# A wait inside each projection in place of a pacing wait in front of it, in a fused sequence-mixing and expert kernel

## Chip, cores and metric

The kernel runs on one core of one Trainium2 chip, as one program. The metric is the device time in microseconds of one execution; lower is better.

## What is computed

The input x is (8, 1024, 256) in fp32. Two blocks, each behind a layer norm over the 256 columns and added to x:

```python
def attn(x):                               # (the sequence-mixing half)
    xp, z = split(x @ w_in)                # 256 -> 2 x 512
    xc = silu(causal_conv(xp, 4 taps) + conv_b)
    h_t = 0.9 * h_{t-1} + 0.1 * (xc_t @ w_B)   # state of 16
    return ((h @ w_C) * silu(z)) @ w_out   # "out projection", 512 -> 256

def ffn(x):
    idx = top_2(x[:, 0, :] @ Wr + br)      # per sequence, from its first token
    h = gelu(x @ W1[idx] + b1[idx])        # two experts, 256 -> 256 each
    return mean over the two of (h @ W2[idx] + b2[idx])   # "down projection"

x = x + attn(layernorm(x))
x = x + ffn(layernorm(x))
```

## The kernel before

The 8,192 tokens are cut into 16 chunks of 512 tokens. The kernel is a pipeline over chunks: step s does the sequence mixing of chunk a = s, the out projection of chunk o = s - 1 and the expert half of chunk f = s - 2. Steps 4 to 13 are a hardware loop over pairs of steps, the others are written out. Each engine has its own program of steps; semaphores that count up order them.

Each matrix product is done in split precision: both operands are kept as a high part (fp32r) and the rest, and three products (hi by hi, lo by hi, hi by lo) add up in one bank of PSUM. A product is two instructions of TensorE: a weight load (LDWEIGHTS, 128 x 128, the stationary operand) and a matmul that streams the moving operand. A wait in front of a product is carried by its weight load, an increment by its matmul. The profile shows weight loads as engine PEld and matmuls as PE.

There are two sizes of product. In xp and z (both in_proj), up, state_in and state_out the moving operand is 512 tokens ("long" products, 128x512). In the out projection (out_proj) and the down projection (down) the stationary operand is a tile of 128 tokens and the moving one is a 256-column weight ("short" products, 128x256). These two go through tokens(h, j, ...), where h is a half of the chunk (two tiles of 128 tokens) and j one of four slices of the contraction: six short products for each call, lines 1419 to 1421. A projection is 2 halves x 4 slices x 6 = 48 short products. The out projection runs in one piece; of down the first 36 run in one piece and the last 12 behind state_out.

The order of TensorE in one step is: xp (24 long), out_proj(o, 0) and out_proj(o, 1) (48 short), z (24 long), up (24 long), state_in (8 long), down(f, 0) and the first half of down(f, 1) (36 short), state_out (4 long), the rest of down(f, 1) (12 short). Every other step has six tiny products of the router (score) at its start.

In front of 15 out projections and 15 down projections stands behind(tail, count). The third-last product of the long stream in front counts up a semaphore (x_tail, state_tail or up_tail). TensorE first counts up a semaphore of its own that nobody reads (paced), then waits for the third-last product's end, and then issues PACE = 2 more increments of paced before it comes to the first weight load of the projection.

Of the kernel before, what the change touches and what calls it, by code (L numbers as in the profile page):

```python
# [16 lines left out]
SQ = 32  # L17
QUADS = P // SQ
EARLY = 2
PACE = 2  # L20


def build_block(nc, x, w_in, conv_w, conv_b, w_B, w_C, w_out, Wr, br, W1, b1, W2, b2, out):
# [10 lines left out]
    JD = DI // P  # L34
    JF = TOP_K * KD
# [7 lines left out]
    with ExitStack() as ctx:  # L43
# [3 lines left out]
        def sem(name):  # L47
            return ctx.enter_context(nc.semaphore(name))
# [43 lines left out]
        w_out_hi, w_out_lo = sb("w_out_hi", [P, JD, D], F32R), sb("w_out_lo", [P, JD, D], F32R)  # L92
        w2_hi, w2_lo = sb("w2_hi", [P, TOP_K, KD * D], F32R), sb("w2_lo", [P, TOP_K, KD * D], F32R)
# [6 lines left out]
        y_hi, y_lo = sb("y_hi", [P, JD, CH], F32R), sb("y_lo", [P, JD, CH], F32R)  # L100
        hid_hi, hid_lo = sb("hid_hi", [P, JF, CH], F32R), sb("hid_lo", [P, JF, CH], F32R)
# [35 lines left out]
        t1_hi, t1_lo = sem("t1_hi"), sem("t1_lo")  # L137
        half_turned = sem("half_turned")
        half_hi, half_lo = sem("half_hi"), sem("half_lo")
        t2_hi, t2_lo = sem("t2_hi"), sem("t2_lo")  # L140
# [25 lines left out]
        up_ready = sem("up_ready")  # L166
# [6 lines left out]


        passed = sem("passed")
        x_tail, state_tail, up_tail = sem("x_tail"), sem("state_tail"), sem("up_tail")
        paced = sem("paced")


        raw_in = gate[:].rearrange("p j c -> p (j c)").rearrange("p (k c) -> p k c", k=KD)  # L180
# [90 lines left out]
        def has_attn(s):  # L271
            return not isinstance(s, int) or s <= LAST
# [964 lines left out]
        def _(pe):  # L1237
# [49 lines left out]
                    nc.tensor.transpose(blk[0][:, k * P:(k + 1) * P], by_token(normed2, 0)[:, k * P:(k + 1) * P],  # L1287
                                        ident[:]).then_inc(token_turned, 1)

            def project(bank, whi, wlo, his, los, ready, c, sem_out, third_last=None, between=None):  # L1290

                dst = bank[:]
                for k in range(KD):
                    if ready is not None:
                        pe.wait_ge(ready[0], c * KD + k + 1)
                    mm(dst, whi(k), his(k), start=(k == 0), stop=False)  # L1296
                    ins = mm(dst, wlo(k), his(k), start=False, stop=False)  # L1297
                    if k == 0 and between is not None:
                        between()
                if third_last is not None:  # L1300
                    ins.then_inc(third_last, 1)
                for k in range(KD):
                    if ready is not None:
                        pe.wait_ge(ready[1], c * KD + k + 1)
                    ins = mm(dst, whi(k), los(k), start=False, stop=(k == KD - 1))  # L1305
                ins.then_inc(sem_out, 1)

            def in_proj(a, j, part, bank, sem_out, between=None):
                cols = slice(part * DI + j * P, part * DI + (j + 1) * P)
                project(bank, lambda k: w_in_hi[:, k, cols], lambda k: w_in_lo[:, k, cols],  # L1310
                        lambda k: xn1(a)[0][:, k, :], lambda k: xn1(a)[1][:, k, :],
                        (t1_hi, t1_lo) if part == 0 and j == 0 else None, a, sem_out,
                        x_tail if part == 0 and j == JD - 1 else None, between)

            def last_tap(a, j):
                return a * JD * HALO + (j // 2) * 2 * HALO + 2 * (HALO - 1) + j % 2 + 1
# [53 lines left out]
            def up(s, f, q, seq):  # L1370
                for j in range(JF):
                    if q == 0 and j % KD == 0:
                        pe.wait_ge(w1_lo_set, seq * TOP_K + j // KD + 1)
                    if has_attn(s):
                        pe.wait_ge(gate_set, s * JD + j + 1)
                    elif has_out(s):
                        pe.wait_ge(y_set, NC * JD - JD + j + 1)
                    else:
                        pe.wait_ge(gelu_set, f * JF - JF + j + 1)
                    t, m = j // KD, j % KD  # L1380
                    project(blk[j], lambda k: w1_hi[:, t, k * D + m * P:k * D + (m + 1) * P],
                            lambda k: w1_lo[:, t, k * D + m * P:k * D + (m + 1) * P],
                            lambda k: xn2(f)[0][:, k, :], lambda k: xn2(f)[1][:, k, :],
                            (t2_hi, t2_lo) if j == 0 else None, f, up_ready,
                            up_tail if j == JF - 1 and not has_attn(s) else None)

            def up_first():
                his, los = xn2(0)
# [21 lines left out]
                            lambda k: w1_lo[:, 1, k * D + m * P:k * D + (m + 1) * P],  # L1410
                            lambda k: his[:, k, :], lambda k: los[:, k, :], None, 0, up_ready)

            def tokens(h, j, last, his, los, whi, wlo):


                for n in range(2):
                    rows = slice((2 * h + n) * P, (2 * h + n + 1) * P)
                    dst = tok[h][:, n * D:(n + 1) * D]
                    mm(dst, his[:, j, rows], whi, start=(j == 0 and n == 0), stop=False, skip_group_check=True)  # L1419
                    mm(dst, his[:, j, rows], wlo, start=False, stop=False, skip_group_check=True)  # L1420
                    ins = mm(dst, los[:, j, rows], whi, start=False, stop=(last and n == 1), skip_group_check=True)  # L1421
                return ins

            def behind(tail, count):
                pe.sem_inc(paced, 1)
                pe.wait_ge(tail, count)
                for _ in range(PACE):
                    pe.sem_inc(paced, 1)

            def down_tile(f, n, dst, js=range(JF)):  # L1430
                rows = slice(n * P, (n + 1) * P)
# [5 lines left out]
                if js[-1] == JF - 1:  # L1437
                    ins.then_inc(down_ready, 1)

            def down(f, h, js=range(JF), tail=None):  # L1440
                for j in js:
                    if h == 0:
                        pe.wait_ge(g_lo, f * JF + j + 1)
                        if isinstance(f, int) and f == LAST - 1 and j % KD == 0:
                            pe.wait_ge(w2_lo_set, LAST // 2 * TOP_K + j // KD + 1)
                    if j == 0 and tail is not None:
                        behind(*tail)
                    t, cols = j // KD, slice(j % KD * D, (j % KD + 1) * D)
                    ins = tokens(h, j, j == JF - 1, hid_hi, hid_lo, w2_hi[:, t, cols], w2_lo[:, t, cols])
                if js[-1] == JF - 1:  # L1450
                    ins.then_inc(down_ready, 1)

            def out_proj(o, h, tail=None):
                pe.wait_ge(done, o * 2 + h + 1)
                for j in range(JD):
                    if h == 0:
                        if isinstance(o, int) and o == LAST and j:
                            pe.wait_ge(last_y_lo, j)
                        else:
                            pe.wait_ge(y_lo_set, o * JD + j + 1)  # L1460
                    if j == 0 and tail is not None:
                        behind(*tail)
                    ins = tokens(h, j, j == JD - 1, y_hi, y_lo, w_out_hi[:, j, :], w_out_lo[:, j, :])
                ins.then_inc(mixed, 1)

            def state_in(a):
                bank = u_bank(a)
                for j in range(JD):
                    pe.wait_ge(xc_hi_set, a * JD + j + 1)
                    mm(bank[:], b_mix[:, j, :], xc_hi[:, j, :], start=(j == 0), stop=False)  # L1470
                for j in range(JD):
                    pe.wait_ge(xc_lo_set, a * JD + JD if isinstance(a, int) and a < 3 else a * JD + j + 1)
                    ins = mm(bank[:], b_mix[:, j, :], xc_lo[:, j, :], start=False, stop=(j == JD - 1))  # L1473
                    if j == JD - 3:
                        ins.then_inc(state_tail, 1)
                ins.then_inc(u_ready, 1)

            def state_out(a, s, js=range(JD)):
# [41 lines left out]
            def opening():  # L1520
# [22 lines left out]
                for j in (1, 2, 3):  # L1543
                    xp(2, j)
                pe.wait_ge(z_out_lo_set, 3)
                out_proj(0, 0, (x_tail, 3))
                out_proj(0, 1)
                state_in(1)
                z(2, (0, 1))
# [6 lines left out]
                up_first()  # L1556
                state_in(2)
                pe.wait_ge(y_set, 2 * JD)
                out_proj(1, 0, (state_tail, 3))
                out_proj(1, 1)  # L1560
                pe.wait_ge(w2_lo_set, TOP_K)
                pe.wait_ge(mid_set, 3)
# [8 lines left out]
            def step(s, q, half):  # L1571
# [4 lines left out]
                    for j in range(JD):  # L1576
                        xp(a, j)
                if has_out(s):
                    out_proj(o, 0, (x_tail, a + 1) if has_attn(s) else None)
                    out_proj(o, 1)  # L1580
                if has_attn(s):
                    z(a)
# [10 lines left out]
                else:  # L1593
                    pe.wait_ge(done, f * 2 + 3)
                if not has_out(s):
                    down(f, 0, (0, 1, 2), (up_tail, 2))
                    pe.wait_ge(done, f * 2 + 4)
                    down_tile(f, 2, tok[1][:, 0:D], (0, 1, 2))
                    down(f, 0, (3,))
                    down_tile(f, 2, tok[1][:, 0:D], (3,))  # L1600
                    down_tile(f, 3, turn[0][:, 0:D])
                    return
                if isinstance(s, int) and s == NC:
                    down(f, 0, (0, 1, 2), (up_tail, 1))
                    down(f, 1, (0, 1))
                    down(f, 0, (3,))
                    turns2(o)
                    down(f, 1, (2, 3))
                    return
                down(f, 0, range(JF), (state_tail, a + 1))  # L1610
                down(f, 1, (0, 1))
                if has_attn(s):
                    state_out(a, s)
# [30 lines left out]
```

## Time and profile before

| | us |
|---|---|
| median of 3 runs | 507.03 |
| lowest, highest | 506.91, 507.4 |
| the profiled execution | 507.05 |
| its span, first to last instruction | 505.0 |
| TensorE (PE) busy | 499.6 |
| weight loads (PEld) busy | 438.9 |
| VectorE, ScalarE, GpSimd busy | 452.7, 400.5, 348.1 |

Times of a timeline are us from the start of the span. A matmul's duration in the profile holds its passage through the array, so neighbours overlap: the distance from one start to the next is what a product costs the stream, and the duration is when its result is there. The granted TensorE clock is 1.00 of the upper level over the whole span.

### The profile page before, as it was taken

The numbers are of one execution on the slowest core, as the hardware profiler recorded it, in microseconds if no ns is written. First come the engines' busy times: TensorE is split into PE (matmuls) and PEld (weight loads), VectorE is DVE, ScalarE is ACT, GpSimd is POOL, SyncE is SP. The second block draws the span as 40 slices with busy tenths as digits, with TensorE's granted clock in tenths as the row PEclk, the third lists the DMA queues.
The fourth block names the chain that finished last, engine by engine and source line by source line (L and its number), as shares of the span: only waits on it lengthen the run. The fifth ranks groups of instructions, "written<-read, shape, count | busy, mean of one in ns | idle before, by whom it ended". The sixth has DMA issues, their size and how long they took to land.

```text
span 505.0 us, 9913 instructions
## 1 busy us (share of the span) xinstructions
PE 499.6 (99%) x3026; PEld 438.9 (87%) x3026; DVE 452.7 (90%) x896; ACT 400.5 (79%) x692; POOL 348.1 (69%) x390
## 2 busy tenths in 40 slices
PE   7999999999999999999999999999999999999997
PEld 7888799888888888888889888888888888888997
DVE  6999999999998899989999899998999989996773
ACT  4986959878869788697887969879797888969454
POOL 4959597559693796928969197783977649673391
PEclk9999999999999999999999999999999999999999
DMA  8940105335251532606235170542614333130102
GB/s 255 298 183 5 38 1 178 115 127 168 69 184 42 166 125 83 208 15 196 80 125 166 42 224 25 166 125 86 205 42 139 110 126 126 55 113 1 42 2 84
DMA packets 53379, 57.28 MB, mean 113 GB/s; under 512 B 8682, under 2 KB 49642, under 8 KB 53226
## 3 DMA queue, kind: packets, MB, share of 16 engines
q1 hardware_dynamic: 51498, 56.67, 34.8%
q10 hardware_dynamic: 1856, 0.31, 0.3%
q8 instruction: 12, 0.20, 0.2%
q14 instruction: 13, 0.11, 0.1%
HBM read 35.46 MB, written 21.50 MB: 113 GB/s over the span
## 4 chain that ended last, share of the span: by engine, by line
PE 98%; DVE 1%; DMA 1%; issue 0%; DVEq 0%
PE blk L1296 16%; PE blk L1297 16%; PE blk L1305 16%; PE tok L1419 12%; PE tok L1421 11%; PE tok L1420 11%; PE blk L1494 3%; PE turn L1470 3%; PE turn L1473 3%; PE turn L1243 1%; PE tok L1296 1%; PE tok L1297 1%; PE tok L1305 1%; DMA x_mid<-in_L_attn_x 1%; DVE stats_t L917 0%; DVE normed L934 0%
## 5 line engine op out<-in xcount | busy, mean ns | idle before, releaser
L992 DVE SCALAR_TENSOR_TENSOR conv<-blk,tap_w,conv 128x512 f32<-128x512 f32 x192 | 130.1, 740 | 7.3 <-ACT conv L683 6.4
L488 POOL TENSOR_TENSOR y_lo<-gate,y_hi 128x512 fp32r<-128x512 f32 x57 | 72.2, 1297 | 36.0 <-ACT y_hi L611 35.9
L1296 PE MATMUL blk<-xn_hi,w_in_hi 128*128 128x512 f32 x228 | 89.5, 392 | 0.0
L1297 PE MATMUL blk<-xn_hi,w_in_lo 128*128 128x512 f32 x228 | 89.0, 391 | 0.0
L453 POOL TENSOR_TENSOR xc_lo<-conv,xc_hi 128x512 fp32r<-128x512 f32 x60 | 73.1, 1236 | 7.7 <-ACT xc_hi L611 7.6
L1419 PE MATMUL tok<-w_out_hi,y_hi 128*128 128x256 f32 x256 | 72.3, 282 | 0.0
L1421 PE MATMUL tok<-w_out_hi,y_lo 128*128 128x256 f32 x256 | 70.8, 277 | 0.0
L1420 PE MATMUL tok<-w_out_lo,y_hi 128*128 128x256 f32 x256 | 70.7, 276 | 0.0
L1305 PE MATMUL blk<-xn_lo,w_in_hi 128*128 128x512 f32 x228 | 70.3, 390 | 0.0
L1419 PE MATMUL tok<-w_hi,hid_hi 128*128 128x256 f32 x248 | 70.3, 283 | 0.0
L1420 PE MATMUL tok<-w_lo,hid_hi 128*128 128x256 f32 x248 | 68.9, 278 | 0.0
L1421 PE MATMUL tok<-w_hi,hid_lo 128*128 128x256 f32 x248 | 68.8, 278 | 0.0
L683 ACT ACTIVATE conv<-blk,tap_b,tap_w 128x512 f32<-128x512 f32 x64 | 49.2, 778 | 24.8 <-PE blk L1305 21.6
L689 ACT ACTIVATE conv<-conv 128x512 f32<-128x512 f32 x64 | 39.4, 630 | 30.4 <-DVE conv L992 29.4
L861 DVE TENSOR_TENSOR hid_lo<-hid,hid_hi 128x512 fp32r<-128x512 f32 x64 | 45.1, 731 | 16.0 <-ACT hid_hi L611 15.7
L498 POOL TENSOR_TENSOR x_mid<-x_mid,b_sel 128x256 f32<-128x256 f32 x60 | 45.7, 793 | 13.3 <-DVE hid_lo L861 11.3
L1419 PEld LDWEIGHTS tok<-w_out_hi,y_hi 128*128 128x128 f32 x256 | 48.0, 188 | 3.8 <-issue 3.6
L1305 PEld LDWEIGHTS blk<-xn_lo,w_in_hi 128*128 128x128 f32 x228 | 42.8, 188 | 9.1
L1419 PEld LDWEIGHTS tok<-w_hi,hid_hi 128*128 128x128 f32 x248 | 46.5, 188 | 4.4 <-issue 3.9
L1297 PEld LDWEIGHTS blk<-xn_hi,w_in_lo 128*128 128x128 f32 x228 | 42.8, 188 | 8.1
L1296 PEld LDWEIGHTS blk<-xn_hi,w_in_hi 128*128 128x128 f32 x228 | 42.8, 188 | 8.1
L1296 PE MATMUL blk<-xn_hi,w_hi 128*128 128x512 f32 x124 | 48.4, 390 | 0.0
(189 smaller groups left out, 1319.4 us busy)
## 6 DMA issues: line engine op xcount, KB each, us to landing
spill<-normed SPq DMA_DIRECT2D x25, 512.0 KB, 2.8
normed<-spill SPq DMA_DIRECT2D x100, 128.0 KB, 2.9
out<-x_mid SPq DMA_DIRECT2D x30, 256.0 KB, 2.3
x_mid<-in_L_attn_x SPq DMA_DIRECT2D x29, 256.0 KB, 2.8
x_in<-in_L_attn_x SPq DMA_DIRECT2D x14, 512.0 KB, 4.6
w_all<-in_L_ffn_W SPq DMA_DIRECT2D x2, 2048.0 KB, 11.3
b_all<-in_L_ffn_b SPq DMA_DIRECT2D x1, 1024.0 KB, 13.7
gate<-in_L_attn_w_in SPq DMA_DIRECT2D x2, 256.0 KB, 4.8
```

The costliest lines, as they stand in the source:

```text
L453: nc.gpsimd.tensor_tensor(xc_lo[:, j, :], conv[:, j, 0:CH], xc_hi[:, j, :].bitcast(F32), ALU.subtract).then_inc(xc_lo_set, 1)
L488: nc.gpsimd.tensor_tensor(y_lo[:, j, :], gate_of(o, j), y_hi[:, j, :].bitcast(F32), ALU.subtract).then_inc(y_lo_set, 1)
L498: ins = nc.gpsimd.tensor_tensor(mid(f, q)[:, n, :], mid(f, q)[:, n, :], b2_sel[:], ALU.add)
L683: nc.scalar.activation(conv[:, j, HALO:HALO + CH], blk[j][:], ACT.Identity, bias=tap_b[:, j:j + 1], scale=tap_w[:, j, 0:1]).then_inc(tap_f ...
L861: return nc.vector.tensor_tensor(dst, src, hi.bitcast(F32), ALU.subtract)
L992: nc.vector.scalar_tensor_tensor(cols, blk[j][:], tap_w[:, j, t:t + 1], cols, ALU.mult, ALU.add).then_inc(tap_added, 1)
L1296: mm(dst, whi(k), his(k), start=(k == 0), stop=False)
L1297: ins = mm(dst, wlo(k), his(k), start=False, stop=False)
L1305: ins = mm(dst, whi(k), los(k), start=False, stop=(k == KD - 1))
L1419: mm(dst, his[:, j, rows], whi, start=(j == 0 and n == 0), stop=False, skip_group_check=True)
L1420: mm(dst, his[:, j, rows], wlo, start=False, stop=False, skip_group_check=True)
L1421: ins = mm(dst, los[:, j, rows], whi, start=False, stop=(last and n == 1), skip_group_check=True)
```

## The change

The pacing goes: the three tail semaphores, paced, PACE and behind(), and the arguments that carried them. In its place tokens() gets a semaphore and a count for its first call of a projection (h = 0, j = 0). The first product counts the semaphore up at its end, and the fifth product (the second of the second tile) waits for that count. Products 2, 3 and 4 are issued before that wait. This is done for all 16 out projections (first_out) and all 16 down projections (first_down), so also for the first down and the last out projection, which had no pacing.

```diff
-PACE = 2
...
-        x_tail, state_tail, up_tail = sem("x_tail"), sem("state_tail"), sem("up_tail")
-        paced = sem("paced")
+        first_out, first_down = sem("first_out"), sem("first_down")
...
-            def project(bank, whi, wlo, his, los, ready, c, sem_out, third_last=None, between=None):
+            def project(bank, whi, wlo, his, los, ready, c, sem_out, between=None):
...
-                    ins = mm(dst, wlo(k), his(k), start=False, stop=False)
+                    mm(dst, wlo(k), his(k), start=False, stop=False)
...
-                if third_last is not None:
-                    ins.then_inc(third_last, 1)
...
-            def tokens(h, j, last, his, los, whi, wlo):
+            def tokens(h, j, last, his, los, whi, wlo, first=None, count=None):
...
-                    mm(dst, his[:, j, rows], whi, start=(j == 0 and n == 0), stop=False, skip_group_check=True)
+                    ins = mm(dst, his[:, j, rows], whi, start=(j == 0 and n == 0), stop=False, skip_group_check=True)
+                    if first is not None and n == 0:
+                        ins.then_inc(first, 1)
+                    if first is not None and n == 1:
+                        pe.wait_ge(first, count)
                     mm(dst, his[:, j, rows], wlo, start=False, stop=False, skip_group_check=True)
...
-            def behind(tail, count):
-                pe.sem_inc(paced, 1)
-                pe.wait_ge(tail, count)
-                for _ in range(PACE):
-                    pe.sem_inc(paced, 1)
...
-            def down(f, h, js=range(JF), tail=None):
+            def down(f, h, js=range(JF)):
...
-                    if j == 0 and tail is not None:
-                        behind(*tail)
...
-                    ins = tokens(h, j, j == JF - 1, hid_hi, hid_lo, w2_hi[:, t, cols], w2_lo[:, t, cols])
+                    ins = tokens(h, j, j == JF - 1, hid_hi, hid_lo, w2_hi[:, t, cols], w2_lo[:, t, cols],
+                                 *((first_down, f + 1) if h == 0 and j == 0 else ()))
...
-                    ins = tokens(h, j, j == JD - 1, y_hi, y_lo, w_out_hi[:, j, :], w_out_lo[:, j, :])
+                    ins = tokens(h, j, j == JD - 1, y_hi, y_lo, w_out_hi[:, j, :], w_out_lo[:, j, :],
+                                 *((first_out, o + 1) if h == 0 and j == 0 else ()))
...
-                    if j == JD - 3:
-                        ins.then_inc(state_tail, 1)
...
-                out_proj(0, 0, (x_tail, 3))
+                out_proj(0, 0)
...
-                down(f, 0, range(JF), (state_tail, a + 1))
+                down(f, 0)
```

The other callers change in the same way.

## Rows read from the trace of the kernel before

**Rows 1.** The page, busy time of the engines (share of the span) and instructions.

```profile
PE 499.6 (99%) x3026; PEld 438.9 (87%) x3026; DVE 452.7 (90%) x896; ACT 400.5 (79%) x692; POOL 348.1 (69%) x390
```

**Rows 2.** The page, chain of work that ended last, by engine.

```profile
PE 98%; DVE 1%; DMA 1%; issue 0%; DVEq 0%
```

**Rows 3.** The waits: who waited for whom, total us, times, longest us.

```profile
PEld tok L1419 <- issue: 7.5, 30, 0.4
```

**Rows 4.** Timeline, matmuls, xp, out projection and z of one step: start us, us.

```profile
201.26 0.61 PE L1305 MATMUL blk<-xn_lo,w_in_hi 128*128 128x512 f32 x2
...
203.98 0.62 PE L1305 MATMUL blk<-xn_lo,w_in_hi 128*128 128x512 f32 x2
204.45 0.36 PE L1419 MATMUL tok<-w_out_hi,y_hi 128*128 128x256 f32 x1
204.64 0.28 PE L1420 MATMUL tok<-w_out_lo,y_hi 128*128 128x256 f32 x1
...
205.56 0.28 PE L1419 MATMUL tok<-w_out_hi,y_hi 128*128 128x256 f32 x1
...
209.64 0.28 PE L1419 MATMUL tok<-w_out_hi,y_hi 128*128 128x256 f32 x1
...
209.98 0.40 PE L1296 MATMUL blk<-xn_hi,w_in_hi 128*128 128x512 f32 x1
```

**Rows 5.** Timeline, weight loads at the start of the same out projection.

```profile
203.99 0.19 PEld L1305 LDWEIGHTS blk<-xn_lo,w_in_hi 128*128 128x128 f32 x1
204.41 0.19 PEld L1419 LDWEIGHTS tok<-w_out_hi,y_hi 128*128 128x128 f32 x1 [0.24 <-issue]
```

**Rows 6.** Timeline, matmuls, state_in, 36 products of down, state_out.

```profile
221.80 1.07 PE L1473 MATMUL turn<-xc_lo,b_mix 128*128 128x512 f32 x4
222.71 0.36 PE L1419 MATMUL tok<-w_hi,hid_hi 128*128 128x256 f32 x1
222.91 0.28 PE L1420 MATMUL tok<-w_lo,hid_hi 128*128 128x256 f32 x1
...
226.88 1.09 PE L1494 MATMUL blk<-state_mix,c_mix 128*128 128x512 f32 x4
```

**Rows 7.** Timeline, matmuls, last 12 products of down behind state_out.

```profile
227.80 0.28 PE L1419 MATMUL tok<-w_hi,hid_hi 128*128 128x256 f32 x1
227.92 0.28 PE L1420 MATMUL tok<-w_lo,hid_hi 128*128 128x256 f32 x1
...
229.22 0.17 PE L1502 MATMUL turn<-spread_hi,token_hi 128*1 128x8 f32 x1
```

**Rows 8.** Timeline, matmuls, the 36 products of down in step 15.

```profile
465.65 0.36 PE L1419 MATMUL tok<-w_hi,hid_hi 128*128 128x256 f32 x1
465.84 0.28 PE L1420 MATMUL tok<-w_lo,hid_hi 128*128 128x256 f32 x1
...
469.96 0.63 PE L1494 MATMUL blk<-state_mix,c_mix 128*128 128x512 f32 x2
```

**Rows 9.** Timeline, a late operand in front of state_out, and down behind it.

```profile
134.61 1.01 DVE L861 TENSOR_TENSOR state_mix<-state,state_mix 64x512 fp32r<-64x512 f32 x1 [0.20 <-ACT state_mix L611]
...
135.68 0.30 PEld L1494 LDWEIGHTS blk<-state_mix,c_mix 128*128 128x128 f32 x2
...
136.72 0.28 PE L1419 MATMUL tok<-w_hi,hid_hi 128*128 128x256 f32 x1
...
137.96 0.28 PE L1421 MATMUL tok<-w_hi,hid_lo 128*128 128x256 f32 x1
```

**Rows 10.** Timeline, matmuls, the last out projection.

```profile
476.29 0.39 PE L1419 MATMUL tok<-w_out_hi,y_hi 128*128 128x256 f32 x1
476.51 0.28 PE L1420 MATMUL tok<-w_out_lo,y_hi 128*128 128x256 f32 x1
...
477.92 0.28 PE L1420 MATMUL tok<-w_out_lo,y_hi 128*128 128x256 f32 x1
```

More of the change, by code:

```diff
@@ L1311, in in_proj @@
                         lambda k: xn1(a)[0][:, k, :], lambda k: xn1(a)[1][:, k, :],
-                        (t1_hi, t1_lo) if part == 0 and j == 0 else None, a, sem_out,
-                        x_tail if part == 0 and j == JD - 1 else None, between)
+                        (t1_hi, t1_lo) if part == 0 and j == 0 else None, a, sem_out, between)
             def last_tap(a, j):
@@ L1383, in up @@
                             lambda k: xn2(f)[0][:, k, :], lambda k: xn2(f)[1][:, k, :],
-                            (t2_hi, t2_lo) if j == 0 else None, f, up_ready,
-                            up_tail if j == JF - 1 and not has_attn(s) else None)
+                            (t2_hi, t2_lo) if j == 0 else None, f, up_ready)
             def up_first():
@@ L1445, in down, with out_proj @@
                             pe.wait_ge(w2_lo_set, LAST // 2 * TOP_K + j // KD + 1)
-                    if j == 0 and tail is not None:
-                        behind(*tail)
                     t, cols = j // KD, slice(j % KD * D, (j % KD + 1) * D)
-                    ins = tokens(h, j, j == JF - 1, hid_hi, hid_lo, w2_hi[:, t, cols], w2_lo[:, t, cols])
+                    ins = tokens(h, j, j == JF - 1, hid_hi, hid_lo, w2_hi[:, t, cols], w2_lo[:, t, cols],
+                                 *((first_down, f + 1) if h == 0 and j == 0 else ()))
                 if js[-1] == JF - 1:
                     ins.then_inc(down_ready, 1)
-            def out_proj(o, h, tail=None):
+            def out_proj(o, h):
                 pe.wait_ge(done, o * 2 + h + 1)
@@ L1460, in out_proj @@
                             pe.wait_ge(y_lo_set, o * JD + j + 1)
-                    if j == 0 and tail is not None:
-                        behind(*tail)
-                    ins = tokens(h, j, j == JD - 1, y_hi, y_lo, w_out_hi[:, j, :], w_out_lo[:, j, :])
+                    ins = tokens(h, j, j == JD - 1, y_hi, y_lo, w_out_hi[:, j, :], w_out_lo[:, j, :],
+                                 *((first_out, o + 1) if h == 0 and j == 0 else ()))
                 ins.then_inc(mixed, 1)
@@ L1558, in opening @@
                 pe.wait_ge(y_set, 2 * JD)
-                out_proj(1, 0, (state_tail, 3))
+                out_proj(1, 0)
                 out_proj(1, 1)
@@ L1578, in step @@
                 if has_out(s):
-                    out_proj(o, 0, (x_tail, a + 1) if has_attn(s) else None)
+                    out_proj(o, 0)
                     out_proj(o, 1)
@@ L1595, in step @@
                 if not has_out(s):
-                    down(f, 0, (0, 1, 2), (up_tail, 2))
+                    down(f, 0, (0, 1, 2))
                     pe.wait_ge(done, f * 2 + 4)
@@ L1603, in step @@
                 if isinstance(s, int) and s == NC:
-                    down(f, 0, (0, 1, 2), (up_tail, 1))
+                    down(f, 0, (0, 1, 2))
                     down(f, 1, (0, 1))
```

## Prediction, made before the changed kernel was run

> **What bounds the kernel.** I read the busy shares first. TensorE is busy for 499.6 of 505.0 us [rows 1], and the chain that ended last is 98% TensorE [rows 2]. No other engine sets the pace over a stretch of any length, so a nanosecond gained or lost between two products is gained or lost at the end. Then I asked the waits for the weight-load side. The only wait that returns all through the run is the one that the change touches: the load of the first L1419 product was idle 30 times, 7.5 us in total, with no data to blame ("issue") [rows 3]. That is 0.25 us each, but the load side is always idle for 0.04 us per 512-column product (loads of 0.19 us, products 0.227 us apart), and products overlap loads. So the 7.5 us are not the price. The price has to be read from product starts.
>
> The timeline gives two units. Products of 512 columns start 2.72 / 12 = 0.2267 us apart (201.26 to 203.98), and products of 256 columns start 4.08 / 36 = 0.1133 us apart (205.56 to 209.64) [rows 4]. From the start of the L1305 pair at 203.98 to the first product of z at 209.98 there are two long and 48 short products. They should take 2 x 0.2267 + 48 x 0.1133 = 5.89 us and took 6.00. **Each paced out projection loses 0.11 us.** It is visible where: the first load starts 0.42 us after the load before it [rows 5], and the second product starts 0.19 us after the first [rows 4]. For a paced down projection: from 221.80 to 226.88 there are four long and 36 short products, 0.907 + 4.080 = 4.987 us, and it took 5.08. **0.09 us** [rows 6]. I take 0.10 for each of the 30.
>
> The second thing to see is that short products have two rhythms. The last 12 products of down(f, 1) follow directly on the four long products of state_out, with nothing held, and take 229.22 - 227.80 = 1.42 us, 0.118 us each [rows 7]. Such entries come 13 times behind state_out; 12 of them are at 0.118 and one at 0.113. Of the 30 paced entries, 29 settle at 0.113 within about five products, and one stays slow for all its 36 products: (469.96 - 465.84) / 35 = 0.118 [rows 8]. The difference of 0.0045 us is per product, so a slow out projection of 48 loses 0.216 us and a slow run of 36 loses 0.16. The granted clock is at its upper level (2.4 GHz) in all of these, so it is not the clock. The pace buys the quick rhythm with 0.10 us.
>
> **The change, part by part.**
>
> 1. Removed: the wait for the third-last product and two semaphore instructions behind it, at 30 places; with them goes the late first load. Three of the 30 started late for their data anyway (the one behind 130.5 us by 0.2 us), so 27 x 0.10 = 2.7 us can come back at most. The increments on the third-last products cost nothing and save nothing: the rhythm of 0.227 runs through them [rows 4].
>
> 2. What an entry costs with nothing held: the first short product behind state_out starts at 227.80, where the fourth long one started at about 226.88 + 3 x 0.229 = 227.57, so after 0.23 us, and the next follows 0.12 later [rows 6, 7]. So 0.003 us, and 3 x 0.0045 = 0.014 us for the three intervals up to the fourth product if they are slow.
>
> 3. Added: the fifth product's load waits for the first product's end, 16 out and 16 down projections. A short product lasts 0.28 us in these rows [rows 7]. A load that waits for another engine starts about 0.06 us after that end: DVE ended at 134.61 + 1.01 = 135.62, the load came at 135.68 [rows 9]. So the fifth load is free 0.34 us after the first product's start. Without the wait it would start with the fourth product, at 3 x 0.1133 = 0.34 in the quick rhythm or 3 x 0.118 = 0.354 in the slow one. The wait ends just when its load is due. Lower bound of its cost: nothing. Upper bound: a full restart as now, 0.19 - 0.11 = 0.08 us [rows 4], if the release is later than that of another engine. The value is near the lower one, as 0.34 against 0.34 says; I take 0.01, and 0.01 for settling. Behind the waiting load stand only TensorE's own products; while it waits, products 2 to 4 run and hide it. The computing of its count is an instruction more that those three products cover too. The increment rides on a product, as above: nothing.
>
> 4. The rhythm afterwards, the disputed term. Rows 9 are the 13th entry behind state_out: there the first load of state_out was held for the DVE until 135.68, and the 12 short products that follow go from 136.72 to 137.96 in 1.24 / 11 = 0.113. A load held in the midst of the first out projection, at 43.3 us, also left 0.113 behind it. Against that, one held at 476.29 was followed by 0.118 (476.51 to 477.92, 12 intervals) [rows 10]. With the paced entries that makes 31 of 33 held starts quick, and 12 of 12 unheld entries behind a stream of long products slow. (Of three unheld entries behind transposes two were slow and one quick.) The fifth load is held, if barely; so I take quick.
>
> The sum: 27 x (0.10 - 0.003 - 0.014 - 0.02) = 27 x 0.063 = 1.7 us, and 0.1 us of the slow 36 at 465.65 if that one turns quick. 1.8 us in all. The profiled execution took 507.05 us (505.0 of span and 2.05 around it), the median is 507.03: 507.0 - 1.8 = **505.2**. The first down projection and the last out projection are not paced now and get the new wait: nothing for 0.01 us each.
>
> **Rivals.**
>
> *B, the wait is over before it can act, and the projections run slow.* It is the same arithmetic read strictly: a wait whose end comes at 0.34 holds nothing that is due at 0.354, so the entry is an unheld one, and 12 of 12 of those were slow. All other held starts in this trace were held by 0.1 us or more. Then an out projection costs 0.216 + 0.003 in place of 0.10 (+0.12) and a down projection's 36 products 0.16 + 0.003 (+0.065): 15 x 0.185 = 2.8 us, plus some 0.2 for the three sites whose pace was hidden. **510.0.** It decides if the fifth load starts with the fourth product and the rhythm behind it is 0.118. Against it: the 12 entries follow only four long products, which were themselves not yet in their rhythm (0.23 apart), where the entries here follow 24 or 56 settled ones; none of those is unheld in this trace.
>
> *C, the two kinds part.* Outs slow and downs quick: 15 x 0.12 - 15 x 0.06 = +0.9, 507.9. Outs quick and downs slow: 15 x 0.065 - 15 x 0.06 = +0.1, 507.1. The rhythm follows from small offsets, and the two kinds have different streams in front, so it can be.
>
> *D, the rhythm is quick from the first product and the wait costs nothing.* Then all of it comes back: 27 x 0.10 + 0.16 = 2.9 us, **504.1**. The mechanism is that a load is always covered by the product before it, so that nothing but the late first load was lost. The Trainium skill says so: "TensorE: Matmul & The Clock Gate", in its sections on the gap between issues and on LDWEIGHTS, puts a load of 128 columns at about 107 ns and a 256-column product at about 109, which leaves a load no way to be the bound. The trace does not agree where nothing is held, with 0.118 in rows 7 against 0.113 in rows 4, and so this gets little.
>
> *E, the fifth load comes late and the loss moves from the first product to the fifth.* 0.08 + 0.037 = 0.12 us a site against 0.10 now: 30 x 0.02 = +0.6, 507.6.
>
> **Chances.** The forecast A 0.36, D 0.12, B 0.33, C 0.12, E 0.07. About 0.2% (1.0 us) is what a measurement of this kernel can tell from no change. A and D are faster, save for a small part of A with a smaller gain: 0.47. C with quick outs, E and that part: 0.18. B and the rest of C: 0.35. The predicted time is that of A; its own range is 504.6 to 506.0. B is too likely to be left out, so the range goes from D to B: 504.0 to 510.1.
>
> **What would show it.** In the profile of the changed kernel, the idle time of L1419's loads on "issue" (7.5 us, 30 times) goes. The first short product starts 0.23 us behind the last long one and the second 0.12 after it: step 2. The fifth product's load starts within 0.36 us of the first product: step 3; at 0.42 or more it is E. From the tenth to the last product of an out projection the mean interval is 0.1133 (A, D) or 0.118 (B): step 4. The forecast is wrong if that interval is 0.118 while the fifth load was not late.

## The result and the profile after

The changed kernel takes 508.76 us (508.58 to 510.16, 8 runs) against 507.21 for the kernel before in the same comparison (506.47 to 507.75, 8 runs). The ratio is 1.0033, with a 95% interval of 1.0023 to 1.0043: a third of a per cent slower. The profiled execution took 508.75 us with a span of 507.0, 2.0 more than before. The granted clock is 1.00 throughout, as before.

The page of the changed kernel, busy time of the engines, answers to [rows 1]. TensorE is still the bound, with 2.3 us more of busy time for the same 3026 products:

```profile
PE 501.9 (99%) x3026; PEld 446.5 (88%) x3026; DVE 452.0 (89%) x896; ACT 401.2 (79%) x692; POOL 347.7 (69%) x390
```

Its waits no longer have the line of [rows 3], L1419's loads on "issue". The timeline shows the entry of the same out projection as in [rows 4], matmuls first: start us, duration us.

```profile
204.38 0.61 PE L1301 MATMUL blk<-xn_lo,w_in_hi 128*128 128x512 f32 x2
204.83 0.28 PE L1413 MATMUL tok<-w_out_hi,y_hi 128*128 128x256 f32 x1
204.95 0.28 PE L1418 MATMUL tok<-w_out_lo,y_hi 128*128 128x256 f32 x1
205.07 0.28 PE L1419 MATMUL tok<-w_out_hi,y_lo 128*128 128x256 f32 x1
205.19 0.28 PE L1413 MATMUL tok<-w_out_hi,y_hi 128*128 128x256 f32 x1
205.31 0.28 PE L1418 MATMUL tok<-w_out_lo,y_hi 128*128 128x256 f32 x1
...
210.49 0.40 PE L1294 MATMUL blk<-xn_hi,w_in_hi 128*128 128x512 f32 x1
```

Its weight loads, where before there was the late one of [rows 5]:

```profile
204.61 0.19 PEld L1413 LDWEIGHTS tok<-w_out_hi,y_hi 128*128 128x128 f32 x1
204.84 0.19 PEld L1418 LDWEIGHTS tok<-w_out_lo,y_hi 128*128 128x128 f32 x1
204.96 0.19 PEld L1419 LDWEIGHTS tok<-w_out_hi,y_lo 128*128 128x128 f32 x1
205.07 0.19 PEld L1413 LDWEIGHTS tok<-w_out_hi,y_hi 128*128 128x128 f32 x1
205.19 0.19 PEld L1418 LDWEIGHTS tok<-w_out_lo,y_hi 128*128 128x128 f32 x1
```

The entry is what the prediction wanted: the first load comes in its turn, the first short product 0.22 us behind the last long one, the second 0.12 later. The fifth load, the one with the wait, starts at 205.19 together with the fourth product. It is not late at all. But the step from one product to the next is 0.118: (210.49 - 204.83) / 48 = 0.1179, where [rows 4] had 0.1133 from the fifth interval on. From the pair at 204.38 to z it is 6.11 us against 6.00. The down projection's 36 products answer to [rows 6]:

```profile
222.30 1.07 PE L1463 MATMUL turn<-xc_lo,b_mix 128*128 128x512 f32 x4
223.21 0.28 PE L1413 MATMUL tok<-w_hi,hid_hi 128*128 128x256 f32 x1
223.32 0.28 PE L1418 MATMUL tok<-w_lo,hid_hi 128*128 128x256 f32 x1
...
227.45 1.09 PE L1482 MATMUL blk<-state_mix,c_mix 128*128 128x512 f32 x4
```

5.15 us against 5.08. All 32 projections of the changed kernel run at 0.118 from their entry on. Two things differ on the way. The first out projection goes over to 0.113 in its midst, behind a load that was held for its data at 43.0 us. Two groups of the last twelve products of down are quick, one at 136.8 us (the same group as in [rows 9], here not held) and one at 491.5 us behind transposes.

### The profile page after: what moved, and what is told of

It reads as the page before. It is cut to its first block, busy times and chain, and to the rows that moved or that the text cites. A ratio compares the mean times of both kernels' runs of the same rounds, so it can differ in the third digit from the quotient of the medians.

```text
span 507.0 us, 9839 instructions
## 1 busy us (share of the span) xinstructions
PE 501.9 (99%) x3026; PEld 446.5 (88%) x3026; DVE 452.0 (89%) x896; ACT 401.2 (79%) x692; POOL 347.7 (69%) x390
## 4 chain that ended last, share of the span: by engine, by line
PE 98%; DVE 1%; DMA 1%; issue 0%; DVEq 0%
PE blk L1294 16%; PE blk L1295 16%; PE blk L1301 16%; PE tok L1419 12%; PE tok L1413 12%; PE tok L1418 12%; PE blk L1482 3%; PE turn L1460 3%; PE turn L1463 3%; PE turn L1241 1%; PE tok L1294 1%; PE tok L1295 1%; PE tok L1301 1%; DMA x_mid<-in_L_attn_x 1%; DVE stats_t L915 0%; DVE normed L932 0%
## 5 line engine op out<-in xcount | busy, mean ns | idle before, releaser
L1419 PE MATMUL tok<-w_out_hi,y_lo 128*128 128x256 f32 x256 | 71.9, 281 | 0.0
L1418 PE MATMUL tok<-w_out_lo,y_hi 128*128 128x256 f32 x256 | 71.9, 281 | 0.0
L1419 PE MATMUL tok<-w_hi,hid_lo 128*128 128x256 f32 x248 | 69.7, 281 | 0.0
L1418 PEld LDWEIGHTS tok<-w_out_lo,y_hi 128*128 128x128 f32 x256 | 49.0, 191 | 0.6
L1418 PEld LDWEIGHTS tok<-w_lo,hid_hi 128*128 128x128 f32 x248 | 47.5, 191 | 1.1
```

## The experiments

In the list, "late" is how long after its turn a load starts, its turn being the start of the product before it. Times are medians, spans are those of the profiled execution.

The trace holds times in ns, which the printed rows round to 0.01 us; where a difference of a few ns matters, it is given in ns. "Quick" is a step of 0.1133 us from product to product, "slow" one of 0.118.

**1 and 2: does the wait do anything, and is it the wait or its lateness?** Two kernels that hold nothing in effect. The first is the changed kernel without its wait:

```diff
-                    if first is not None and n == 1:
-                        pe.wait_ge(first, count)
```

> The changed kernel without the wait in front of the fifth product (the increment stays): nothing is held in front of or inside a projection. If the wait of the change is over before its load is due and so does nothing (theory N), the time is that of the changed kernel, 508.8 within 0.3 us, and all short products are 0.118 us apart. If the wait does some of its work (theory H, the rhythm would be even worse or more often slow without it), it is slower than the changed kernel by 0.5 us or more.

The second is the kernel before with the wait kept and the increments gone:

```diff
-PACE = 2
+PACE = 0
```

> The kernel before with PACE = 0: the wait for the third-last long product's end stays, the two increments behind it go. That wait ends about 0.445 us after the third-last product's start and the first load is due at 0.456, so it should hold nothing. Theory N (a wait that is over in time does nothing): slow rhythm, as the changed kernel, 508.8. Theory Q (emptying the queue of issued instructions is what brings the quick rhythm, late load or not): quick rhythm without the loss of 0.1 us a site, about 504.5.

Measured: 508.69 us (508.58 to 508.74; ratio to the kernel before 1.0036, interval 1.0023 to 1.0050) with a span of 506.9, and 508.74 us (508.50 to 509.09; 1.0038, 1.0024 to 1.0051) with a span of 507.0. Both are the changed kernel to within 0.1 us, with 0.118 from the entry on at all 32 projections. So theory N holds twice: a wait that ends before the load's turn changes nothing, whether it stands in front of the first product or of the fifth. Theory Q, that the wait brings the quick rhythm by emptying the queue of issued instructions, late load or not, would have given about 504.5, and is out as far as this wait does empty the queue, which no row shows.

**3: a late load with no loss.** `PACE = 1`.

> The kernel before with PACE = 1: the first load comes some 0.05 to 0.12 us after it is due, against 0.20 with PACE = 2. A long product gives its successor's load 0.11 us of slack, so TensorE's stream should hardly be interrupted. Theory L (a late load is enough to set the quick rhythm): quick, and most of the 0.1 us a site comes back, 504.3 to 505.5. Theory S (the stream itself must be interrupted): slow rhythm, 508.8.

Measured: 509.01 us (508.89 to 509.88; ratio 1.0044, interval 1.0030 to 1.0057). The weight loads at the entry, and the products:

```profile
205.25 0.41 PEld L1305 LDWEIGHTS blk<-xn_lo,w_in_hi 128*128 128x128 f32 x2
205.76 0.19 PEld L1419 LDWEIGHTS tok<-w_out_hi,y_hi 128*128 128x128 f32 x1
```

```profile
205.48 0.62 PE L1305 MATMUL blk<-xn_lo,w_in_hi 128*128 128x512 f32 x2
205.94 0.28 PE L1419 MATMUL tok<-w_out_hi,y_hi 128*128 128x256 f32 x1
206.05 0.28 PE L1420 MATMUL tok<-w_out_lo,y_hi 128*128 128x256 f32 x1
...
211.59 0.40 PE L1296 MATMUL blk<-xn_hi,w_in_hi 128*128 128x512 f32 x1
```

The load comes 0.51 us after the first of the pair's loads where two turns are 0.45, so some 0.05 late, and costs the stream less than 0.01 us. (211.59 - 205.94) / 48 = 0.118. Slow, and so are all 30 sites, one of them with a first load 0.69 us late for its data (the down projection at 132.4 us; this is the execution of 509.88). A late load is not enough (theory L is out).

**4: interrupt the stream.** The changed kernel with the wait at the fourth product instead of the fifth:

```diff
+                    if first is not None and n == 1:
+                        pe.wait_ge(first, count)
                     ins = mm(dst, his[:, j, rows], whi, start=(j == 0 and n == 0), stop=False, skip_group_check=True)
                     if first is not None and n == 0:
                         ins.then_inc(first, 1)
-                    if first is not None and n == 1:
-                        pe.wait_ge(first, count)
```

> The changed kernel with the wait one product earlier, at the fourth: its load is due 0.24 us after the first product's start and is free at 0.34, so it is 0.10 us late and interrupts the stream. If a late load inside the projection sets the quick rhythm: 0.10 + 0.02 us lost a site and 0.118 turned into 0.113 behind it, so about as before, 507.0 to 507.8. If it does not, the loss is added to the changed kernel's: 508.8 + 32 x 0.10 = 512.0.

Measured: 511.63 us (511.46 to 511.66; ratio 1.0094, interval 1.0078 to 1.0110), the second of the two: the rhythm is slow at every projection. Matmuls of an out projection, with the fourth at 206.13 waiting for its load:

```profile
205.78 0.28 PE L1415 MATMUL tok<-w_out_hi,y_hi 128*128 128x256 f32 x1
...
206.13 0.37 PE L1415 MATMUL tok<-w_out_hi,y_hi 128*128 128x256 f32 x1
206.34 0.28 PE L1418 MATMUL tok<-w_out_lo,y_hi 128*128 128x256 f32 x1
...
211.52 0.40 PE L1294 MATMUL blk<-xn_hi,w_in_hi 128*128 128x512 f32 x1
```

0.09 us are lost at the fourth product, and behind it (211.52 - 206.34) / 44 = 0.118. An interruption of the stream is not enough either, and my count of held starts in the trace of before (31 of 33 quick) did not mean what I took it for.

**5 to 8: the size of the delay.** What was left was theory T, a threshold, against theory P, that the exact offset at which the stream restarts decides. Four sizes: `PACE = 3`; the wait of the kernel before on the second-last long product with `PACE = 0`; and the changed kernel with one and with two increments of an unread semaphore behind its wait:

```diff
                     if first is not None and n == 1:
                         pe.wait_ge(first, count)
+                        for _ in range(1):        # 2 in the other
+                            pe.sem_inc(paced, 1)
```

> The kernel before with PACE = 3, one increment more than the 2 that give the quick rhythm and two more than the 1 that gives the slow one. The first load is then some 0.28 us late (0.05 with one, 0.20 with two). Theory T (beyond a threshold a late first load always gives the quick rhythm): 0.1133 us a product in out and down, and the stream loses 0.08 us more a site, 30 x 0.08 = 2.4: a span of 507 to 507.5. Theory P (the offset at which the stream restarts decides, and 0.20 is one of several that are good): the rhythm may be either, and where it is slow the span is 510 or more.

> The kernel before with PACE = 0 and the wait on the second-last long product in place of the third-last: no increments of paced behind the wait, but the first load comes 0.445 - 0.227 = 0.22 us late, about as late as with PACE = 2 (0.20). If lateness is what counts and not the increments (theories T and P with a broad window): quick rhythm and 507.0 to 507.8. If the exact offset counts (P with a narrow window), 0.015 us may be enough for the slow rhythm: 0.22 + 0.11 us a step more than the changed kernel, 511.5.

> The changed kernel with one increment of a semaphore that nobody reads between the wait and the fifth product's load. By the run with PACE = 1 that makes the load some 0.064 us later, so 0.045 us after it is due. Theory T: still below a threshold, slow rhythm and 32 x 0.045 = 1.4 us more than the changed kernel's span of 507.0, 508.4. Theory P: either rhythm; if quick, the out projections gain 43 x 0.0045 and the downs 31 x 0.0045, 504.3.

> The same with two increments, by the runs with PACE = 1 and 2 some 0.20 us after the load is due. Theory T: as with PACE = 2 quick from there on, 32 x 0.20 us lost (a short product gives no slack for it) and 32 x 0.17 gained against the changed kernel: a span of about 508. Theory P: either rhythm; slow gives 507.0 + 32 x 0.20 = 513.4.

Measured: 512.83 us (one run); 506.97 us (506.30 to 507.30, ratio 0.9995, interval 0.9985 to 1.0004); 506.06 us (one run, span 504.2); 513.47 us (one run). With what was there already:

| kernel | load | late by, us | projections quick / slow |
|---|---|---|---|
| changed, without wait, PACE = 0 | 5th, none, 1st | 0 | none / all |
| PACE = 1 | 1st | 0.05 | none / all |
| one increment at the fifth | 5th | 0.04 | 30 / 1 |
| wait at the fourth | 4th | 0.10 | none / all |
| before (PACE = 2) | 1st | 0.20 (26 sites), 0.23 to 0.40 (4) | 29 / 1 |
| wait on the second-last | 1st | 0.22 | all / none |
| two increments at the fifth | 5th | 0.19 to 0.20 | 8 / 23, both in one execution |
| PACE = 3 | 1st | 0.35 | 19 / 11, both in one execution |

(A few sites are held longer, for their data. The last out projection waits for data between its slices and changes its rhythm on the way; it is not told apart here. Quick or slow is read from the intervals right behind the held load.) More delay is not better: with PACE = 3 ten sites fewer are quick than with PACE = 2. Theory T is out.

The one slow site of "one increment at the fifth" is the first down projection, in both executions that were profiled (this one and that of experiment 9). It follows directly on an out projection that is quick, and enters quick; its fifth load is 0.05 late where the others are 0.04. The expectation of experiment 9 has this trace as quick at all 32 sites, which it was not. Matmuls of this projection, from the trace of experiment 9:

```profile
69.56 0.28 PE L1414 MATMUL tok<-w_hi,hid_hi 128*128 128x256 f32 x1
...
69.90 0.28 PE L1414 MATMUL tok<-w_hi,hid_hi 128*128 128x256 f32 x1
70.01 0.33 PE L1421 MATMUL tok<-w_lo,hid_hi 128*128 128x256 f32 x1
70.18 0.28 PE L1422 MATMUL tok<-w_hi,hid_lo 128*128 128x256 f32 x1
...
72.30 0.28 PE L1422 MATMUL tok<-w_hi,hid_lo 128*128 128x256 f32 x1
```

(69.90 - 69.56) / 3 = 0.113 in front of the held product, (72.30 - 70.18) / 18 = 0.118 behind it. So a held load can also turn a quick stream slow.

PACE = 3 shows how fine it is. An out and a down projection of one step, matmuls:

```profile
205.74 0.61 PE L1305 MATMUL blk<-xn_lo,w_in_hi 128*128 128x512 f32 x2
206.35 0.36 PE L1419 MATMUL tok<-w_out_hi,y_hi 128*128 128x256 f32 x1
206.55 0.28 PE L1420 MATMUL tok<-w_out_lo,y_hi 128*128 128x256 f32 x1
...
212.08 0.39 PE L1296 MATMUL blk<-xn_hi,w_in_hi 128*128 128x512 f32 x1
```

```profile
223.89 1.07 PE L1473 MATMUL turn<-xc_lo,b_mix 128*128 128x512 f32 x4
224.96 0.36 PE L1419 MATMUL tok<-w_hi,hid_hi 128*128 128x256 f32 x1
225.15 0.28 PE L1420 MATMUL tok<-w_lo,hid_hi 128*128 128x256 f32 x1
...
229.14 0.63 PE L1494 MATMUL blk<-state_mix,c_mix 128*128 128x512 f32 x2
```

The first is slow, (212.08 - 206.55) / 47 = 0.1177. The second is quick, (229.14 - 225.15) / 35 = 0.1140 with its settling. The first short product of the slow one starts 387 ns behind the last long product, that of the quick one 385 ns. This holds for all 30 sites: at the 19 with the step of 0.1133 the distance is 385 ns, at the 11 with 0.118 it is 386 or 387 ns (or, at two that were late for their data, 476 and 478). One or two ns part the two rhythms here.

**9: the version that loses least, timed.** The kernel with one increment at the fifth load.

> The kernel of the single look with one increment between the wait and the fifth load, timed. Its trace showed the quick rhythm at all 32 sites and about 0.058 us lost a site against 0.10 before. If that holds in every execution: 30 x 0.04 = 1.2 us less than before, 0.1 of it given back in two sites that were not paced, so 505.9 to 506.2. If the good look was luck (an offset that falls either way from run to run): between that and the changed kernel, 507.4 or more, with a wide spread.

Measured: 506.16 us (505.52 to 506.62, 11 runs) against 506.78 for the kernel before beside it (506.25 to 507.67, 15 runs): ratio 0.9986, interval 0.9977 to 0.9995. It is ahead of the kernel before by a little more than the measurement's doubt, and some 2.5 us ahead of the changed one. It is quick at 30 of the 31 sites told apart, as in the table. Its matmuls:

```profile
204.53 0.28 PE L1414 MATMUL tok<-w_out_hi,y_hi 128*128 128x256 f32 x1
...
205.00 0.32 PE L1421 MATMUL tok<-w_out_lo,y_hi 128*128 128x256 f32 x1
205.15 0.28 PE L1422 MATMUL tok<-w_out_hi,y_lo 128*128 128x256 f32 x1
...
210.04 0.40 PE L1295 MATMUL blk<-xn_hi,w_in_hi 128*128 128x512 f32 x1
```

The fifth product, at 205.00, is 0.04 us longer, waiting for its load, and 48 products take 5.51 us, 0.07 over 48 x 0.1133 = 5.44. Before, an out projection lost 0.11 and a down 0.09. 15 x (0.04 + 0.02) = 0.9 us would come back; the span is 0.6 shorter (504.4).

**10: the same delay in another place, and 11: another delay in the same place.** In the tenth the second product's load waits for the second-last long product's end, with one increment behind the wait. In the eleventh the changed kernel's fifth load waits for the second product's end:

```diff
                     mm(dst, his[:, j, rows], whi, start=(j == 0 and n == 0), stop=False, skip_group_check=True)
+                    if tail is not None and n == 0:          # tenth
+                        pe.wait_ge(*tail)
+                        pe.sem_inc(paced, 1)
...
-                    mm(dst, his[:, j, rows], wlo, start=False, stop=False, skip_group_check=True)
+                    ins = mm(dst, his[:, j, rows], wlo, start=False, stop=False, skip_group_check=True)
+                    if first is not None and n == 0:         # eleventh
+                        ins.then_inc(first, 1)
```

> The pacing kernel with the wait moved to the second product's load: it waits for the second-last long product's end and one increment, which makes it some 0.05 us late where a short product leaves no slack. 30 sites. Theory P' (a load that is late by about 0.05 us and delays the stream brings the quick rhythm, wherever in the projection it stands): quick from the second product on, 0.05 to 0.06 us lost a site, 505.8 to 506.2. Theory P (the exact offset decides, and a few ns or another place can change it): slow is as likely, 508.7 + 30 x 0.05 = 510.2.

> The changed kernel with the fifth load waiting for the second product's end in place of the first's: 0.10 us late, as the fourth load was in the run that waited one product earlier, and slow there. If the size of the delay decides and not the product at which it comes: slow rhythm, a span of about 509.8. If the place decides (the fifth is good for 0.04 us): quick, 507.0 + 32 x (0.10 - 0.17) = 504.8.

The eleventh took 511.44 us (one run), with a span of 509.6: slow at 0.10 late, as the fourth kernel was, at 30 of 31 sites. (The first down projection is quick.) The tenth gave two times. One execution, the profiled one, took 506.32 us with a span of 504.5; five took 510.18 to 510.33 with spans of 508.3 to 508.5. Nothing came between. (Ratio over all six 1.0068, interval 1.0054 to 1.0082.)

**12 to 14: the two times.** The tenth kernel profiled again, and the same with one and with three increments of the unread semaphore added once at the start of TensorE's program, behind the first transposes:

> The same kernel as the one that held the second load, profiled once more. One of its six executions took 506.3 us and its profile is quick at all sites; five took 510.2. If the difference is the rhythm (theory P, the offset at which the load restarts falls either way from one execution to the next), a profile of an execution of 510.2 shows the second load as late as the quick one did, to a few ns, and 0.118 us a product behind it. If something else costs the 3.9 us, the products are 0.1133 apart as in the first profile and the time is lost elsewhere.

> The kernel that holds the second load, with one increment of the unread semaphore added once, at the start of TensorE's program. In itself it costs at most 0.07 us. Theory P: 506.3 or 510.2 again, and a profile at 510 (a span of 508.4) has a second load that is late by 0.05 us as before and 0.118 us a product behind it. If the two times are something else, the products of a slow profile are 0.1133 apart.

> The same with three increments at the start, at most 0.2 us in itself. Expected as for one increment: 506.3 to 506.5 with the quick rhythm or 510.2 to 510.4 with the slow one, and nothing between.

Measured: 506.30 us (one run) for the twelfth; 506.18 (505.95 and 506.42) for the thirteenth; 510.30 (510.24 and 510.36, span 508.4) for the fourteenth, which gives a trace of the slow case. The three quick profiles (10, 12, 13) are quick at 29 of 30 held sites each, not at all sites as the expectation of 12 has it; the slow one is slow at all 30. Matmuls of the quick execution of the tenth kernel:

```profile
204.65 0.28 PE L1418 MATMUL tok<-w_out_hi,y_hi 128*128 128x256 f32 x1
204.77 0.32 PE L1422 MATMUL tok<-w_out_lo,y_hi 128*128 128x256 f32 x1
204.93 0.28 PE L1423 MATMUL tok<-w_out_hi,y_lo 128*128 128x256 f32 x1
...
210.16 0.40 PE L1295 MATMUL blk<-xn_hi,w_in_hi 128*128 128x512 f32 x1
```

And of the fourteenth:

```profile
205.45 0.28 PE L1418 MATMUL tok<-w_out_hi,y_hi 128*128 128x256 f32 x1
205.56 0.33 PE L1422 MATMUL tok<-w_out_lo,y_hi 128*128 128x256 f32 x1
205.73 0.28 PE L1423 MATMUL tok<-w_out_hi,y_lo 128*128 128x256 f32 x1
...
211.15 0.40 PE L1295 MATMUL blk<-xn_hi,w_in_hi 128*128 128x512 f32 x1
```

The code of the projections is the same, the second load is late by 0.05 us in both (204.70 for a product at 204.65, 205.50 for one at 205.45), and the held product takes 0.32 and 0.33. In ns the third product starts 277 or 278 behind the first at 28 of the 29 quick sites of the tenth, and 280 at all 30 of the fourteenth. The 48 products take 5.51 and 5.70 us. Behind the held one the quick execution settles at 0.1133, the slow one stays at (211.15 - 205.73) / 46 = 0.118. 0.19 us an out projection, and by the same count 0.14 a down one: 15 x 0.33 = 4.9 us, against 3.9 between the spans. In the seven steps from the out projection at 235 us on the traces part by 0.30 a step. What is missing lies in the steps before: in two of them the quick execution took longer than the slow one (30.81 us against 30.65 from the out projection at 113 us, 30.73 against 30.52 from that at 174 us).

## Why the prediction was wrong

The prediction said 505.2 us, 0.35% faster. It is 0.33% slower. The range held the value only because it went up to rival B, and B is what happened.

**Steps 1 to 3 were right.** (One small miscount in step 1: with the projection of [rows 8], four first loads were later than the pacing made them, 0.23 to 0.40 us, not three.) The late first load is gone with its price, the entry is 0.22 and then 0.12 us, as step 2 had it. Step 3 put the release of the fifth load at 0.34 us behind the first product and its turn at 0.34 to 0.354. The trace has the load at 0.36 (204.83 to 205.19), with the fourth product: not held. That the release comes at 0.34 is borne out by experiment 4, whose fourth load, waiting for the same end, starts there. Without the wait the kernel takes the same time to 0.1 us (experiment 1).

**Step 4 failed: "the fifth load is held, if barely; so I take quick".** Two errors are in it. The first is in the sentence itself: the release was earlier than a turn of the slow rhythm, by step 3's own numbers, and a wait that ends early holds nothing. The second is the inference from 31 quick starts among 33 held ones. They were not 33 witnesses. 26 of them were one and the same delay of 0.20 us, made by PACE = 2, and the experiments show that this size happens to be good. At the first load 0.05 was slow at every site and 0.35 at a third of them; 0.10 was slow at every site of the fourth load and at all but one of the fifth. In place of the 1.7 us that this step was to bring, the runs show 0.118 behind every entry, +0.11 us an out and +0.07 us a down projection. The trace of before held the warning, the projection of [rows 8] and the held load of [rows 10], both held and both slow, and neither with the 0.20 of the pacing (0.23 and 0.15). I counted them as exceptions.

**Rival B was right in mechanism, and too dear.** It said 510.0, 3.0 over; the profiled spans differ by 2.0, the medians by 1.6. Its terms: an out projection +0.12, measured 6.11 - 6.00 = +0.11; a down projection +0.065, measured 5.15 - 5.08 = +0.07. That is 0.18 a step, or 2.7 us over 15 steps, and from the out projection at 174.2 us to that at 447.4 us the traces part by just this: the changed kernel is 0.20 us behind at the first (174.41) and 1.79 at the second (449.15), nine steps later. What B had too dear is the time before. The changed kernel starts its first out projection 0.23 us earlier (40.92 against 41.15), before any projection has run, and gains 0.07 us in the step from 113 to 144 us, where the kernel before had a first load 0.40 us late for its data (the down projection at 131.42). So late data did not add 0.2 us to the loss, as B had it, but hid part of it: a TensorE that arrives later finds the data there. For the step at 113 us the traces bear this out; where the first 0.23 us come from, and the rest of the 0.7 us between 2.7 and 2.0, no run isolates.

**Its doubt was misplaced.** Against B the prediction held that entries behind 24 or 56 settled long products might be unlike the 12 behind four unsettled ones. Experiment 1 shows 0.118 at the out and down projections of every regular step, behind either.

**C, D and E.** C, the two kinds parting, did not happen here, but did with PACE = 3. D took its figures from the Trainium skill ("TensorE: Matmul & The Clock Gate", the sections on the back-to-back issue gap and on LDWEIGHTS): about 107 ns for a load of 128 columns and, as an estimate by its formula for a single product, about 109 ns for 256 columns. That a load is then always covered was D's own conclusion. With nothing held the trace shows 0.118 throughout, and 0.1133 elsewhere with the same instructions; both are above the page's figure, so the conclusion does not hold for these products. E, a late fifth load, needs an increment more; with it the load is 0.04 late, and the result is a gain of 0.14% on the kernel before (experiment 9), not E's loss.

**What is not settled.** The runs show that the rhythm is set at the entry or the restart and kept for up to 48 products. With PACE = 3 one or two ns part the two cases, and two or three ns between the tenth kernel and the fourteenth; that these ns are the cause, and not a second mark of it, is argued. With two increments at the fifth load no such distance separates the 8 sites at 0.1133 from the 23 at 0.118. What inside TensorE has the two rhythms was not tried. Nor is it known why both profiled executions of the tenth kernel were quick and its other five were not. Profiling alone does not explain it: the thirteenth was quick with and without it, the fourteenth slow both times.

## What to carry to other kernels

When a stream of equal products has two rhythms, read the step from product to product at every site first, and find how each was entered. A delay that happens to set the good one is a matter of its exact size: scan the size (none, one, two, three increments) and time several executions, since the same program can come out either way, as the tenth kernel did with 506.3 and 510.2 us. A wait is only worth its name if its release is later than the load's turn; work out both times before counting on it, and take many copies of one delay as one observation.

## What was not expected of the hardware

TensorE runs a stream of 128x256 fp32r products, each with its own weight load, either 0.1133 or 0.118 us apart, with the same instructions at the same granted clock, and keeps to the one it entered until a load is held. A weight load that waits for a semaphore which comes up in time costs nothing measurable: 508.69 without the wait and 508.76 with it. One increment between wait and load puts the load some 0.06 us later (0.04 late where it was 0.02 early); with a second the load was 0.19 late, so the second added 0.15. In front of the first product it is the same: 0.05, 0.20 and 0.35 late with one, two and three.
